# A last edge pass that picks each block's rows by products, and a first attention walk that ends at step 244

## What is computed

```python
h = relu(layernorm(x)); x = x + L0(h)   # two mean-of-neighbours layers, elu, log_softmax
h = relu(layernorm(x)); x = x + L1(h)   # attention with 4 heads, batch norm, feed-forward
h = relu(layernorm(x)); x = x + L2(h)   # attention with 2 heads, prelu
h = relu(layernorm(x)); x = x + L3(h)
# L3: msg = h[src] @ weight[rel] + bias[rel]          (4 relations)
#     agg = segment_max(msg, dst), 0 where a node has no edge
#     L3  = h @ weight[4] + bias[4] + agg
```

## Time and profile before

| | |
|---|---|
| median of 3 runs | 5873.93 us (5870.14 to 5876.07) |
| time of the profiled execution | 5876.16 us |
| its span, first to last instruction | 5874.4 us, mean granted clock 0.728 |
| busy | POOL 3903.4 us (66%), PE 3278.1 (56%), DVE 2906.4 (49%), ACT 1827.9 (31%) |
| DMA | 474.71 MB, mean 81 GB/s |

### The profile page before, as it was taken

How to read it: one execution, slowest core, us unless ns; L and a number is a source line. 1 busy time by engine, 2 the same in 40 slices (tenths; PEclk the granted TensorE clock), 3 DMA queues, 4 the chain that set the end, 5 groups by cost and what they waited for, 6 DMA issues and landing times. The chain is left out here.

```text
span 5874.4 us, 89970 instructions
## 1 busy us (share of the span) xinstructions
PE 3278.1 (56%) x15772; PEld 2756.8 (47%) x15773; DVE 2906.4 (49%) x7625; ACT 1827.9 (31%) x6493; POOL 3903.4 (66%) x4083
## 2 busy tenths in 40 slices
PE   3444555545555525889999894244555563334332
PEld 3444455444555523677777644233445533333331
DVE  4233344434455656788888852344555652222221
ACT  2111111111122213666666653233344441111110
POOL 4777777677777747777776003777777517777776
PEclk9667777766677756999999995566677785555555
DMA  4222222211111112344444211222222134444443
GB/s 122 61 62 63 63 65 66 72 53 52 53 53 52 53 41 78 111 113 117 119 117 113 95 46 31 52 53 54 53 53 52 38 111 130 133 132 130 131 133 107
DMA packets 441899, 474.71 MB, mean 81 GB/s; under 512 B 131954, under 2 KB 337214, under 8 KB 441695
## 3 DMA queue, kind: packets, MB, share of 16 engines
q0 software_dynamic: 130464, 264.37, 17.1%
q1 hardware_dynamic: 184116, 146.31, 8.3%
q10 hardware_dynamic: 127227, 63.09, 3.6%
HBM read 315.46 MB, written 157.97 MB: 81 GB/s over the span
## 5 line engine op out<-in xcount | busy, mean ns | idle before, releaser
L1194 PE MATMUL pa<-arena,weighted 128*128 x4480 | 860.0, 367 | 855.8 <-POOLq L913 511.2
L1194 PEld LDWEIGHTS pa<-arena,weighted 128*128 128x128 f32 x4480 | 795.4, 273 | 909.4 <-issue 909.2
L422 POOL DMA_INDIRECT arena<-y_tab,slot x784 | 739.8, 944 | 398.7 <-issue 209.4
L1607 POOL DMA_INDIRECT arena<-t_tab,src_idx x784 | 777.5, 992 | 265.7 <-issue 216.0
L919 POOL DMA_INDIRECT arena<-h_tab,src_idx x784 | 742.8, 947 | 308.1 <-issue 221.9
L2490 POOL DMA_INDIRECT arena<-t_tab,src_idx x784 | 753.3, 961 | 244.9 <-issue 224.6
L919 POOL DMA_INDIRECT arena<-sage_tab,src_idx x784 | 739.8, 944 | 262.4 <-issue 216.1
L471 DVE TENSOR_TENSOR_SCAN scan_t<-mask,scan_t,pa 128x512 f32<-128x512 bf16 x196 | 250.9, 1280 | 737.1 <-PE pa L495 737.1
L495 PE MATMUL pa<-ident,arena 128*128 128x128 f32 x784 | 218.3, 434 | 603.9 <-DMA arena<-y_tab,slot 603.9
L495 PEld LDWEIGHTS pa<-ident,arena 128*128 128x128 f32 x784 | 140.1, 217 | 681.9 <-DMA arena<-y_tab,slot 430.8
L2731 PE MATMUL pa<-weighted 128*128 128x130 f32 x2240 | 422.6, 364 | 21.0 <-ACT weighted L2809 11.0
(11 more groups left out here) (522 smaller groups left out, 6559.9 us busy)
## 6 DMA issues: line engine op xcount, KB each, us to landing
gat_tab<-out_rows SPq DMA_DIRECT2D x248, 260.0 KB
scan_rows<-out_rows ACTq DMA_DIRECT2D x196, 256.0 KB, 3.7
arena<-t_tab,src_idx POOLq DMA_INDIRECT x1568
mask<-cut_row SPq DMA_DIRECT2D x196, 128.0 KB, 3.1
arena<-h_tab,src_idx POOLq DMA_INDIRECT x784
arena<-sage_tab,src_idx POOLq DMA_INDIRECT x784
y_tab<-arena SPq DMA_DIRECT2D x49, 256.0 KB, 2.3
arena<-y_tab,slot POOLq DMA_INDIRECT x784, 2.8
```

Source lines behind the costliest of these rows:

```text
L422: nc.gpsimd.indirect_dma_start(out=rows(c, t), out_offset=None, in_=table[:, :], in_offset=bass.IndirectOffsetOnAxis(ap=slot[:, c, t:t + 1 ...
L1194: ins = nc.tensor.matmul(pa[:, b * CE:b * CE + RW], hot[b][:, t * P:(t + 1) * P], ring[:, bass.ds(start + t * RW, RW)], start=(t == 0), st ...
L1607: nc.gpsimd.indirect_dma_start(out=rows[:, g % QR * QT + t, :], out_offset=None, in_=t1_tab[:, :], in_offset=bass.IndirectOffsetOnAxis(ap= ...
```

## The change

1. `edge_pass` and `gather_results` go. In their place stands a walk of 160 steps like L0's. `staged_t`, `run_t` and `kept_t` have two buffers, `back_ps` and `last_ps` one. For step s: ScalarE copies the group's 896 rows out of the ring (`stage_group`), TensorE transposes them (`turn`), VectorE scans 896 columns (`scan`) and carries the last column over (`carry_on`, two one-column instructions), TensorE transposes back (`back`), ScalarE copies the result to SBUF (`keep_back`), VectorE builds the zero-one matrices, in which a one now stands only at the last edge of each node (`build`), TensorE multiplies (`select`), VectorE adds the product to x (`add`), and ScalarE issues a store of the block before (`store`) and the load of the mask (`load_mask`). A ring place is free once the copy out of it is done. Ahead of the walk the tables for it are made; GpSimd issues two more indirect DMAs behind the third group, and waits there for `last_rows` to be stored. `scan_rows` is no more.
2. In `project`, VectorE's order in a step is front(i+2), post(i) in all cases. TensorE's turn(i+1) and ScalarE's keep(i+1) stand ahead of all seven blocks of group i, and the products go round two PSUM banks.
3. L1's walk runs `QL` = 244 steps; the last window has 4 (`fine_steps`). It has its own `group_col1` and `block_col1`, since the last pass uses `group_col` and `block_col` of L0 once more.
4. In the setup some memsets, one load and the index of last edges go.

The core of the diff:

```diff
                     def step(i, b, left):
-                        if left > 1 and starts is None:
+                        if left > 1:
                             front(dve, i + 2)
                         dve.wait_ge(group_product.sem, group_product.past(i + 1))
                         post(dve, i, b)
-                        if left > 1 and starts is not None:
-                            front(dve, i + 2)
...
-                                if t == 4 and left > 0:
-                                    turn(i + 1)
...
-                                pe.wait_ge(tile_out.sem, tile_out.by_last_lap(i * NG + (max(t, 1) if t < 3 else max(t - 1, 2))))
-                                to = banks[t % 4][:, 0:n]
+                                pe.wait_ge(tile_out.sem, tile_out.by_last_lap(i * NG + (t + 1 if t > 1 else 2 - t)))
+                                to = pb[:, t % 2 * CE:t % 2 * CE + n]
...
-                        if left > 0 and by_tile is None:
+                        if left > 0:
                             turn(i + 1)
-                        multiply(i, b, left)
+                        multiply(i, b)
...
-                        if left > 0 and by_tile is None:
+                        if left > 0:
                             keep(i + 1, 1 - b)
...
-                with sp.Fori(0, QS // 2) as pair:
+                with sp.Fori(0, QL // 2) as pair:
...
-                    for q in range(QW):
+                    for q in range(fine_steps(w)):
...
-        edge_pass(y_tab, D, y_idx, cut_row, ALU.add, ALU.max)
...
+            @block.vector
+                def scan(s, b):
+                    after(dve, edge_turned, s + 1)
+                    after(dve, mask_loaded[b], (s - b) * 8 + 16)
+                    after(dve, edge_back, s - 1)
+                    after(dve, carry_ready, s)
+                    v.tensor_tensor_scan(run_t[b], mask_t[b], turned_ps[b], carry_t[b], ALU.add, ALU.max).then_inc(edge_scanned.sem, 1)
...
+                def body(i, b):
+                    if inside(i):
+                        scan(i, b)
+                    if inside(i - 2):
+                        add(i - 2, b)
+                    if inside(i):
+                        carry_on(i, b)
+                        build(i, b)
...
+            @block.tensor
+                def turn(s, b):
+                    after(pe, edge_staged, s + 1)
+                    after(pe, edge_scanned, s - 1)
+                    for t in range(GT):
+                        ins = nc.tensor.transpose(turned_ps[b][:, t * P:(t + 1) * P], staged_t[b][:, t * P:(t + 1) * P], ident[:, :])
+                    ins.then_inc(edge_turned.sem, 1)
+                def back(s, b):
+                    after(pe, edge_scanned, s + 1)
+                    after(pe, edge_kept, s)
+                    for t in range(GT):
+                        ins = nc.tensor.transpose(back_ps[:, t * P:(t + 1) * P], run_t[b][:, t * P:(t + 1) * P], ident[:, :])
+                    ins.then_inc(edge_back.sem, 1)
+                def select(s, b):
+                    after(pe, edge_kept, s + 1)
+                    after(pe, hot_built, s + 1)
+                    after(pe, block_added, s)
+                    for t in range(GT):
+                        ins = nc.tensor.matmul(last_ps, hot[b][:, t * P:(t + 1) * P], kept_t[b][:, t * P:(t + 1) * P],
+                                               start=(t == 0), stop=(t == GT - 1))
+                    ins.then_inc(block_summed.sem, 1)
+                def body(i, b):
+                    if inside(i + 1):
+                        turn(i + 1, 1 - b)
+                    if inside(i - 1):
+                        select(i - 1, 1 - b)
+                    if inside(i):
+                        back(i, b)
...
+            @block.scalar
+                def body(i, b):
+                    if not isinstance(i, int) or 0 <= i < SN + 2:
+                        j, start, need = window_values(mybir.EngineType.Activation, scalar_walk, i, 0, STEP)
+                    if inside(i) and inside(i + 2):
+                        load_mask(i + 2, b, need)
+                    if inside(i):
+                        keep_back(i, b)
+                    if inside(i - 2):
+                        store(i - 2, j)
+                    if inside(i) and inside(i + 2):
+                        stage_group(i + 2, b, start, need)
```

More of the change, by code:

```diff
@@ L167, in build @@
         block_col = sb("block_col", [P, 2])
+        group_col1 = sb("group_col1", [P, 2], I32)
+        block_col1 = sb("block_col1", [P, 2])
         last_dst = sb("last_dst", [GN, 1], I32)
@@ L250, in build @@
         sums_ready = count("sums_ready")
-        gathered = [count(f"gathered{c}") for c in range(NB)]
-        idx_staged = count("idx_staged")
+        iota_made = count("iota_made")
         hot_made = [count(f"hot_made{a}", 2 * LQ) for a in range(2)]
@@ L319, in build @@
         cuts_kept = count("cuts_kept")
[L320 to L325, removed]
+        edge_staged = count("edge_staged")
+        edge_turned = count("edge_turned")
+        edge_scanned = count("edge_scanned")
+        edge_back = count("edge_back")
+        edge_kept = count("edge_kept")
+        carry_held = count("carry_held")
+        carry_ready = count("carry_ready")
+        mask_loaded = [count(f"mask_loaded{b}") for b in range(2)]
         group_staged = count("group_staged")
@@ L564, in results_gathered @@
-        def results_gathered():
-            for b in range(2):
-                group_rows[b].base += 16 * NG * ((groups + 1 - b) // 2)
-            group_here.base += groups
         def stage(s):
@@ L608, in project @@
             with nc.Block() as block:
-                if gathers is not None:
-                    @block.gpsimd
-                    def _(pool):
-                        gathers(pool)
                 if starts is not None:
@@ new lines, in _, with stage_group, load_mask, keep_back @@
+            @block.scalar
+            def _(act):
+                def stage_group(s, b, start, need):
+                    after(act, edge_turned, s - 1)
+                    wait_apart(act, group_landed.sem, group_landed.past(need))
+                    nc.scalar.copy(staged_t[b].rearrange("p (t d) -> p t d", d=D),
+                                   ring[:, bass.ds(start, GT * RW)].rearrange("p (t w) -> p t w", w=RW)[:, :, 0:D]
+                                   ).then_inc(edge_staged.sem, 1)
+                def load_mask(s, b, need):
+                    after(act, edge_scanned, s - 1)
+                    act.dma_start(mask_t[b], cut_row[0:1, bass.ds((need - 1) * GE, GE)].broadcast_to([P, GE])).then_inc(mask_loaded[b].sem, 16)
+                def keep_back(s, b):
+                    after(act, edge_back, s + 1)
+                    after(act, block_summed, s - 1)
+                    nc.scalar.copy(kept_t[b], back_ps).then_inc(edge_kept.sem, 1)
+                def store(s, j):
+                    after(act, block_added, s)
+                    after(act, block_stored, s * 16)
+                    act.dma_start(out[bass.ds(j * P, P), :], x[:, bass.ds(j, 1), :].rearrange("p j d -> p (j d)")
+                                  ).then_inc(block_stored.sem, 16)
+                STEP = [(0, NT - 2), (0, (RG - 1) * GT * RW), (1, GN)]
+                def body(i, b):
[9 more added lines that the diff above has]
+                        stage_group(i + 2, b, start, need)
+                act.wait_ge(walk_laid.sem, walk_laid.past(1))
+                for s in range(2):
+                    start, need = loaded_values(mybir.EngineType.Activation, pe_walk[0:1, s, :], STEP[1:3])
+                    load_mask(s, s, need)
+                    stage_group(s, s, start, need)
+                walk_steps(act, body)
+                act.wait_ge(block_stored.sem, block_stored.past(SN * 16))
```

376 lines of the change are left out of this document (159 added, 217 removed).

## The result

The changed kernel takes 5932.47 us in the median of 4 runs (5924.97 to 5935.78), the kernel before 5872.03 us (4 runs). The ratio is 1.010, with a 95% interval from 1.0083 to 1.0118: slower by about 60 us, where 5863 us, faster by 9, was forecast. The profiled execution has a span of 5923.2 us against 5874.4.

The account below looks back on a forecast made before the run. POOL's gather issue was taken to bound the old last pass. From the profiled 5876.2 us, less 45 for small parts and 1058.4 for the old pass, plus 1092 for the new: 5864.8, median 5863; range 5805 to 5950.

Parts of the forecast that it names:

- The small parts: L1's walk, the three projections, setup and tables, all ahead of the last pass: together 45 us less.
- L1's projection: VectorE's wait before `post` is covered by the new order and POOL then bounds: 13.4 us less.
- L2's projection: Cycle from `post` to `post` falls from 14.1 to 9.9 us: 15.5 us less, range -17 to +3.
- L3's gave: L3's projection, VectorE's order unchanged: net 1 us less, range -8 to +20.
- The chain: New last walk: back, keep_back, stage_group, turn, select, next back close on themselves, leaving TensorE a 2.1 us gap each step.
- The formula for the pass: Last pass: maximum over edge share x of 8.73(112x + 2) + C(160 - 112x - 49x²), plus 16; 1092 us.
- C: Time of one step of the new last walk: 6.2 us at an assumed TensorE clock of 0.80.
- 104 us of gain: Gain set against last-walk steps that no gather hides; from C = 6.3 on the kernel was to be slower.
- The rival on the other side: Last walk with worse clock or hops, C = 6.8 to 7.2: 5927 us at 6.8, 5952 at 7.0; chance 0.25.
- The clock stays high: Last walk with C = 5.4 to 5.6, POOL bounding for two thirds: 5806 to 5812 us; chance 0.23.
- TensorE at 1.2 GHz throughout: Last walk at the old pass's clock of 0.50, C = 8.4: some 6150 us; chance 0.04.
- The projections did gain: Its rival: projections do not gain, the chain merely starting elsewhere; 28 us missing, 5892 us; chance 0.06.

Follow-up runs that it names:

- filled kernel: The changed kernel plus 7 useless identity products of TensorE behind each `back`: 5807.51 us, ratio 0.988; a second version with 14 transposes instead: 5804.9 us, ratio 0.9875.
- the longer gap filled: The changed kernel plus a second, unread copy of `back_ps` in `keep_back` and 11 useless identity products behind each `back`: 5846.93 us, ratio 0.9951.
- the control: The changed kernel with one register operation more ahead of each wait on a loaded number: 5938.41 us, ratio 1.0099.

## Why the prediction was wrong, point by point

**The small parts** were right in sum, 45 forecast and 45.9 by the traces, but not one by one. From the last gather of L0 to the first of L1's walk it was 127.0 us and is 117.9: L1's projection gave 9.1, not 13.4. The scatters start 2.2 us later and stand back to back (0.30 us between any two), both as forecast, but some of them take 1.3 to 1.9 us and not 0.98: 67.5 us from first to last, not 63. (With the 63 and the 2.2, 78.9 us give 13.7 and not 13.4.) L2's projection gave more, 19: the first three cycles from `post` to `post` take 9.6, 9.6 and 7.8 us, and from the third group's scatters on POOL's 9.0 bounds, the lower end of the range that I gave, not the 9.9 that I took. First to last scatter takes 64.4 us, near 49 times 1.29. L3's gave 3, not 1. L1's walk ends 22.6 us sooner, of which 10.7 is its earlier start; the 14.0 of four steps are there from its last gather on, and 2.1 were lost in its gathers.

**The chain** was right: its links, their order and the gap (2.02 to 2.08 us for 2.1). Terms measured: keep 0.91, stage 0.94 (1.05 estimated), hops 0.17 (0.15, for which no row had been given), scan 2.08 (2.2), VectorE with room, and the mask not late. At full clock the step is 5.42, and 5.4 to 5.5 had been forecast.

**The formula for the pass** was right. With C = 6.82 it gives 1159 us, and 1153.1 was measured; with the filled kernel's 5.42 it gives about 1030, and from 4782.4 to 5808.6 it took 1026; with the 6.04 of the longer gap filled it gives 1077, and from 4768.2 to 5840.0 it took 1072. That the tables delay the first scan to 4815.0, 27 us behind the first group's arrival, cost nothing: the walk had caught up with the gathers by its tenth step. One reading of it was wrong: POOL was to wait for released groups from about group 60 on, and did so from group 89. At C = 6.2 the formula has the steps fall behind at group 52, and I added only the 8 places of the ring. But beyond that point the steps fall behind by only a few tenths of a microsecond for each group at first, so the ring takes many groups to fill. Worked through step by step by the formula's own rule, an estimate, the first waits of over 2 us come at about group 105 with C = 6.2, and at about 86 with 6.82.

**The step that failed is the size of C**, the term for a step: 6.2 taken, 6.82 measured. By the formula the 0.62 is worth 67 us; the pass was missed by 61 (94.7 more measured, 33.6 forecast). (The median was missed by 70: the profiled execution lies 7.5 us under the median of the changed kernel, and 2.2 above had been taken.) C failed by how the low clock was priced. I spread it evenly over the step, the gap included: at clock 0.80 TensorE's 3.3 us of work became 4.1. But a low stretch in a gap costs nothing, and here it doesn't lie in the gap. The low clock costs 1.40 us a step. Work of 3.3 us takes 6.3 at clock 0.50, so each microsecond of low clock on the work costs 0.48, and 1.40 ask for 2.9 us of it. A clock of 0.77 means a low share of 0.46 of the time, 3.1 us a step. So nearly all of it fell on the work. Priced like this, C = (2.1 + 3.3)/(1 - 0.48 x low share), an estimate from the same rows: 6.7 at the clock of 0.80 that I took, 6.9 at 0.77. So most of the miss, some 0.5, is the way of pricing, and the clock itself, 0.77 for 0.80, is the smaller part, some 0.2; together they come to a little more than the 0.62 measured. The slow turn, half-slow select and fast back in the step shown above, and the slow back in the other, are the same thing seen directly.

Three figures beside it don't come out of their own terms. At clock 0.70 my way gives 6.7, not 7.0. The "104 us of gain" should be 45 + 81 = 126, which is what makes C = 6.3 the point of no gain. And at C = 5.4 the formula gives 5800, not 5806.

**The rivals.** The rival on the other side had C = 6.8 and 5927 us, nearly the time measured, but for a lower clock (0.70) or a later ScalarE, and neither came: its number was right by luck. I had given it a chance of 0.25. "The clock stays high" is what the filled kernels showed it to be worth: 5807 us, as it said (5806 to 5812), or 5802 by its ratio. TensorE at 1.2 GHz throughout did not occur. The projections did gain.

**What stays open** is what sets the share of low clock. Idle time of TensorE in each step, the mean step, and the clock between 5400 and 5700 us were, by kernel: 0.6 us, 5.42 and 1.00; 1.45, 5.42 and 0.99; 2.05, 6.82 and 0.77 (2.1, 6.85 and 0.79 in the control); 2.35, 6.79 and 0.82; 2.7, 6.82 and 0.88. Above 2 us more idle time went with more clock. What changed was how often a low stretch fell into the walk: it left one or two steps of nine or ten short in the changed kernel, one of three or four at 2.35 us, and every other one at 2.7. What a slow step costs over a full-clock step of the same kernel hardly changed: some 1.7 us (7.1 against 5.4), 1.6 (7.3 against 5.66) and 1.59 (7.62 against 6.03). Each edit that lengthened the gap also lengthened the full-clock step, so the runs don't tell one from the other, and they don't show the law.

## What to carry to other kernels

Where a step is a ring through two engines, look at what the other engine does inside the ring and could do before it: two lines in another order turned 1% slower into 1.7% faster, since ScalarE's staging didn't need what it stood behind. When you price a burst of TensorE behind a gap from the mean clock of a stretch, put all of the low share on the work first; the mean counts the gap too, and here the work had nearly all of the low part. And before a transfer-bound loop is given a chain, work out at which rate transfers free the steps over the whole run: here steps came at 8.7 us at the start and were wanted at 4.7 at the end, so a step of 6.8 looked free and wasn't.

## What the runs showed of the hardware that I had not expected

Idle gaps of 2.05 us in each step went with a granted clock of 0.77 to 0.79, gaps of 1.45 us with 0.99, and useless work in the gap made the kernel 2.2% faster. Fourteen fp32 transposes in the gap held the clock at 1.00 just as 7 products did. A longer gap can go with a higher clock: 0.88 at 2.7 us against 0.77 at 2.05. Copies of ScalarE right behind one another start 0.80 us apart though each takes 0.91.
